# Last stage of a vision tower on one core: four orders of work changed (normalising, transposes, gather loads, low part)

## What is computed

```python
h = layer_norm(x, ln_in_g, ln_in_b)
gate = softmax((h @ router_w + router_b) / TEMP)
vals, idx = top_k(gate, 2)
mix = sum over the two chosen experts of val * (silu(h @ ew1[e] + eb1[e]) @ ew2[e] + eb2[e])
shared = (silu(h @ sw1 + sb1) @ sw2 + sb2) * 0.25
moe_out = mix + shared
fh = layer_norm(moe_out, ff_ln_g, ff_ln_b)
ff_out = silu(fh @ ff_w1 + ff_b1) @ ff_w2 + ff_b2
return x + moe_out + ff_out
```

## Time and profile before

| | us |
|---|---|
| three runs | 931.93, 933.02, 935.03 (median 933.02) |
| profiled execution | 935.13 |
| its span, first to last instruction | 933.3 |
| TensorE busy in the span | 875.3 (94%) |
| VectorE, ScalarE, GpSimd busy | 669.5, 596.8, 435.5 |
| start of the last stage's first up-projection | 798.04 |
| last matmul ends | 924.97 |

### The profile page before, as it was taken

How to read it: one execution, slowest core, us unless ns; L and a number is a source line. 1 busy time by engine, 2 the same in 40 slices (tenths; PEclk the granted TensorE clock), 3 DMA queues, 4 the chain that set the end, 5 groups by cost and what they waited for, 6 DMA issues and landing times. The chain is left out here.

```text
span 933.3 us, 22329 instructions
## 1 busy us (share of the span) xinstructions
PE 875.3 (94%) x5920; PEld 796.6 (85%) x5920; DVE 669.5 (72%) x2240; ACT 596.8 (64%) x1064; POOL 435.5 (47%) x374
## 2 busy tenths in 40 slices
PE   2999999999999999998897999999999999799996
PEld 2788888888888888887786999999999998688885
DVE  8468888787888878885755777776777774766671
ACT  3466667677776676676854666666666665567774
POOL 7012445554555555552641555665665564333330
PEclk9899999999999999999987999999999999899999
DMA  9999999999999988664167788888888873133321
GB/s 221 220 208 221 233 248 245 250 254 251 248 253 236 235 232 221 167 199 150 59 165 236 220 246 254 246 249 253 246 253 248 234 213 119 48 101 101 101 87 44
DMA packets 193915, 186.96 MB, mean 200 GB/s; under 512 B 16413, under 2 KB 168314, under 8 KB 193626
## 3 DMA queue, kind: packets, MB, share of 16 engines
q1 hardware_dynamic: 182784, 166.24, 68.2%
q0 software_dynamic: 9376, 19.42, 6.4%
q10 hardware_dynamic: 1722, 0.93, 0.5%
HBM read 150.48 MB, written 36.04 MB: 200 GB/s over the span
## 5 line engine op out<-in xcount | busy, mean ns | idle before, releaser
L1426 PE MATMUL bank<-xf,wp 128*128 128x256 f32 x1280 | 310.4, 391 | 5.4 <-ACT xf L628 5.4
L1426 PEld LDWEIGHTS bank<-xf,wp 128*128 128x128 f32 x1280 | 235.5, 190 | 47.5 <-issue 4.1
L911 POOL DMA_INDIRECT y_tok<-region,dsti x160 | 164.1, 1026 | 133.2 <-DVE region L1249 97.9
L869 POOL TENSOR_TENSOR rstd<-var,neghalf 128x4 f32<-128x4 f32 (+2 forms) x51 | 76.3, 1496 | 270.5 <-DVE var L1022 140.3
L628 ACT ACTIVATE xf<-region 128x1024 f32<-128x1024 f32 x160 | 174.0, 1136 | 19.8 <-DVE region L942 19.8
L885 POOL DMA_INDIRECT z_rows<-z,posg x130 | 157.2, 1209 | 45.5 <-issue 44.9
L1625 PE MATMUL bank<-region 128*128 128x128 f32 x1280 | 157.2, 276 | 0.0
L1625 PEld LDWEIGHTS bank<-region 128*128 128x128 f32 x1280 | 151.4, 193 | 0.0
L792 ACT ACTIVATE region<-bank,cols 128x256 f32<-128x256 f32 x320 | 126.1, 476 | 22.3 <-PE bank L1614 21.4
L1614 PE MATMUL bank<-parts 128*128 128x256 f32 x960 | 136.0, 291 | 0.3 <-DVE parts L1268 0.2
L942 DVE COPY region<-region 32x1792 f32<-32x1792 f32 x96 | 105.9, 1103 | 42.2 <-ACT hT L648 20.1
(11 more groups left out here) (179 smaller groups left out, 1213.8 us busy)
## 6 DMA issues: line engine op xcount, KB each, us to landing
region<-in_x SPq DMA_DIRECT2D x384, 196.0 KB
region<-in_L_ffn_ew SPq DMA_DIRECT2D x160, 256.0 KB
region<-z_rows SPq DMA_DIRECT2D x80, 130.0 KB, 2.7
region<-y_tok SPq DMA_DIRECT2D x16, 512.0 KB, 5.3
out<-region SPq DMA_DIRECT2D x65, 64.0 KB
ht_dram<-hT SPq DMA_DIRECT2D x16, 256.0 KB, 7.0
r_dram<-rr SPq DMA_DIRECT2D x16, 256.0 KB, 6.9
region<-ht_dram SPq DMA_DIRECT2D x16, 256.0 KB, 6.0
```

The source lines that it names most:

```text
L869: pool.tensor_tensor(dst, var, neghalf[:, 0:var.shape[1]], ALU.pow).then_inc(ready, 1)
L911: pool.indirect_dma_start(y_tok, bass.IndirectOffsetOnAxis(dsti[n % 2][:, i:i + 1], 0), yout[n % 2][:, i], None).then_inc(y_free[n % 2], 16)
L1426: ins = pe.matmul(out_cols, wp[:, s], cols_in, start=s == 0, stop=s == MAIN - 1)
```

## The change

Four places of the last stage, nothing else:

1. ACT: z_norm(q+1) stood between the first silu and the other three; it now stands ahead of all four.
2. PE: t_z(q+1) stood between the two halves of ff_down(q); it now stands between ff_up(q) and an undivided ff_down(q).
3. SP: in step q the load of group q+4 stood ahead of store_out(q); now it is the load of group q+5. The load of group 4 and that of group 5 so stand ahead of every store.
4. DVE: h4_low(q+1) stood behind out3(q-1); it now stands ahead of it.

```diff
@@ SP
             def step3(q, k, h):
-                load_gat(q + 4, k)
+                load_gat(q + 5, 1 - k)
                 store_out(q)
...
-            for q in range(2, 4):
+            for q in range(2, 5):
                 load_gat(q, q % 2)
-            groups(sp, 0, GROUPS - 4, step3)
+            step3(0, 0, 0)
+            groups(sp, 1, GROUPS - 5, step3)
             load_gat(GROUPS, 0, 1)
-            for q in range(GROUPS - 4, GROUPS):
+            for q in range(GROUPS - 5, GROUPS):
                 store_out(q)
@@ ACT
             def step3(q, k, h, z1=GT, now=GT):
-                ff_silu(q, q * EC, 0, 1, now)
                 if z1:
                     z_norm(q + 1, 1 - k, z1)
-                ff_silu(q, q * EC, 1, EC, now)
+                ff_silu(q, q * EC, 0, EC, now)
                 if z1:
                     z_in(q + 1, z1)
@@ DVE
                     norm(q + 2, m2)
+                if m1:
+                    h4_low(q + 1, m1)
                 if out:
                     out3(q - 1, 1 - k, out)
-                if m1:
-                    h4_low(q + 1, m1)
                 if m2:
                     shift(q + 2, m2)
@@ PE
             def step3(q, k, h, z1=GT, now=GT):
                 ff_up(q, now)
-                ff_down(q, k, 0, EC // 2, now)
                 if z1:
                     t_z(q + 1, z1)
-                ff_down(q, k, EC // 2, EC, now)
+                ff_down(q, k, now)
```

More of the change, by code:

```diff
@@ L1663, in ff_up, with ff_down @@
                     in_parts(bank[FF_BANK[c]][:, 0:nt * P], c, ((fw1h, h4h), (fw1h, h4l), (fw1l, h4h)), nt)
-            def ff_down(q, k, lo, hi, nt=GT):
-                if lo == 0 and not (isinstance(q, int) and q == 0):
+            def ff_down(q, k, nt=GT):
+                if not (isinstance(q, int) and q == 0):
                     pe.wait_ge(out_ready, q)
-                for c in range(lo, hi):
+                for c in range(EC):
                     pe.wait_ge(u_used, q * EC + c + 1)
@@ L1673, in ff_down @@
                                         start=c == 0 and t == 0, stop=c == EC - 1 and t == nt - 1)
-                if hi == EC:
-                    ins.then_inc(ffd_done, 1)
+                ins.then_inc(ffd_done, 1)
             pe.wait_ge(w3_loaded, 48)
```

## The result

| | before | changed kernel |
|---|---|---|
| median of 4 runs (lowest to highest), us | 932.47 (930.64 to 935.03) | 925.83 (922.31 to 927.02) |
| ratio, 95% interval | | 0.9929 [0.9908, 0.9950] |
| profiled execution, us | 935.13 | 922.31 |
| its span, us | 933.3 | 920.5 |
| first up-projection of the last stage | 798.04 | 792.49 |

The changed kernel is **6.6 us faster**. That is outside the range (928.2 to 933.7) on the low side, and on the side of "faster", to which the prediction gave 0.39.

What follows compares the result with a forecast made beforehand. Bound: two DMA engines, nearly without a hole. First packet 815.5 + 0.2, stores 96.6, loads 10.25 x 1.75 = 17.9, no holes: end 930.2 instead of 932.6, -2.4 us, so 930.6 us for the kernel; range 928.2 to 933.7.

Steps and rivals of the forecast that it cites:

- 6.82 us a step without waits: TensorE in the last stage: the length of a step once it never waits, against 7.715 before.
- +0.2 was taken: First store, out3(0) now behind h4_low(2): starts 0.2 us later, with ends of -0.3 and +2.5.
- two engines work nearly without a hole for 117.1 us: Kernel before, stores and gather loads from 815.5 to 932.6: about two DMA engines nearly always busy.
- 1.75 us a load: The two engines' share of a gather load: 19.7 us left after stores and holes, over 11.25 loads.
- 0.06: Idle holes of the two DMA engines per step in the kernel before, in us; 0.8 us in all.
- The low end of the forecast, 929.0: Whole kernel's lowest forecast time, us: first store 0.3 earlier and twice the holes that were read.
- 7.79 a step, TensorE's gain goes nowhere: Last stage: stores and load need 7.79 us a step, so 6.85 us steps build a queue; DMA sets the pace.
- one load less: SP's load ahead of the store: eleven gather loads instead of twelve in the saturated stretch, 1.75 us a load.
- TensorE sets the end: Rival: stores queue away behind, TensorE's chain sets the time, 12.7 us less, 920.3; chance 0.07.
- Half of it: Rival: holes of 0.5 us a step, not 0.06; half of the further gain, 3.5 us, giving 927; chance 0.05.
- Nothing: Rival: load 5 isn't through before the first store, or that store slips by what is saved; 933.0; chance 0.10.
- slower: Rival: out3 behind h4_low makes the first store one step (7.7 us) late; 938; chance 0.03.

Runs made afterwards that it cites:

- a_dve_undone_2: Changed kernel with DVE's part undone (sum again ahead of the low part): 923.19 us, ratio 0.9917; the same kernel on another chip 1002.32 us, 0.9981.
- a_small: Changed kernel with gather loads of one tile of each group instead of four: 997.62 us against 1005.03 before, ratio 0.9958.
- b_sp_only: Kernel before with SP's part of the change alone (load q+5 ahead of the stores of q): 930.94 us against 930.87, ratio 1.0004.
- a_tail_spread: Changed kernel with only the stores of groups 12 to 15 written as two of 64 rows x 4 tiles: 917.69 us, ratio 0.9854.
- a_sp_undone: Changed kernel with SP's part undone, only PE, ACT and DVE as changed: 934.16 us, ratio 1.0034.

## Why the prediction was wrong, point by point

**Right: the chain on TensorE.** It foresaw 6.82 us a step without waits (6.76 to 6.79 measured), the last matmul some 9 us earlier (11.4), 43 GB/s up to the end, and stores issued at 1.4 us each. The first store came 0.8 us sooner where +0.2 was taken and -0.3 was the lower end, in a first step that was 1.0 shorter. It was also right that the last stores and not TensorE end the kernel, and that part of TensorE's gain isn't paid out.

**Wrong: "two engines work nearly without a hole for 117.1 us".** This sentence is on the kernel before; it is the step that failed, and with it the 1.75 us a load. I took every slice that showed some DMA share for work at full capacity, and counted as a hole one slice, at 29 GB/s. The earlier trace rows has three more in the same step, at 38, 31 and 31 where stores alone give 44: by the same way of counting 0.3 us beside the 0.14. But a queue that is given a group each 7.7 us and needs less for it also shows packets in flight most of the time. The measured capacity, from the changed kernel (groups 0 to 10) and from a_dve_undone_2, is 7.30 us a step. Less 4 x 1.51 for the stores, that is **1.25 us a load, not 1.75**, and before the change 7.71 - 7.30, about **0.4 us of rest a step, not 0.06**. The residual of one equation was booked on the one unknown that I had named. A check was at hand in the trace: the time of SP's four issues, which doesn't grow, shown above.

That one term makes up the miss. With 1.25 for 1.75 and all else as it stands, the sum is 815.7 + 96.6 + 10.25 x 1.25 = 925.1 for the last packet, 7.5 us earlier than before, and 925.5 for the kernel, where 925.83 was measured. So the mechanism of the sum, two engines without a hole up to the end, holds for the changed kernel and not for the one before. That it comes so close is in part luck: the limit by the last sums lies at the same place (a_small), the first store was taken 1.0 us too late, and from the first store's packet to the last the trace has 110.6 us where these terms give 109.4. The low end of the forecast, 929.0, should have been about 929.3 by the terms that it names.

**Wrong for that reason: what the step would be.** "7.79 a step, TensorE's gain goes nowhere" became 6.8 for six steps and 7.0 to 7.2 for eight. VectorE wasn't waiting for gathers in the later steps, as I had announced, but for GpSimd. The term "one load less" of 1.75 measured 0 alone (b_sp_only): in that kernel the engines rest, and work taken away adds to the rest.

**What the gain is made of.** TensorE ends 11.4 us sooner: 1.0 in the first step, 10.4 in the 14 others. 4.2 are given back behind it: the distance from the last matmul to the end goes from 8.3 to 12.5. The sum of group 13 stood 13.5 us ahead of the last matmul and stands now 8.4 ahead; the sums behind it follow in 4.9 and 2.1 us where a group's stores take 6.05, and so the stores line up. Left are 7.3 us of stage, 6.6 in the medians.

**The rivals.** "TensorE sets the end" (920) had the pace right and the end wrong; a_tail_spread shows what it would have been, 917.69. "Half of it" (927) named the right doubt, holes of 0.5 us a step where I read 0.06, and came nearest to 925.83; it had 0.05, far too little, since nothing in the trace excluded it: the 0.06 was one slice in two steps. Its number is near by luck as well, since nothing but a guess made it half of the 7 us. "Nothing" and "slower" are out, but a_sp_undone shows how near the second was: without SP's part the change loses 3 us, by gathers held up behind stores and not by a late first store.

## What to carry to other kernels

That packets are in flight doesn't say that a DMA path is full: in the kernel before, fewer than two were in flight for only 1.25 of 89 us, and yet the path had about 0.4 us of rest a step. Set the time at which a group's data is ready beside the time at which its last packet passes: here a constant distance (8.3 to 8.7 us) went with a path that rested, a growing one (8.7 to 10.4) with a path that didn't; the issue time of the held-up queue (3.2 to 4.2 us for four stores, against 3.48 growing to 5.57) showed the same without counting. And a path that keeps up in the loop can still set the end: the last groups, which here come 4.9 and 2.1 us apart where a group's stores take 6.05, are where its width costs, so the last stores of a kernel are the first to be written wide (here four groups of 16 brought as much as all; that was tried only in the changed kernel, whose queue had caught up by group 13, and not in a_dve_undone, whose queue hadn't).

## What the runs showed of the hardware that I hadn't expected

- **A narrow store against a wide one.** A 64 KB store with two images as its outer dimension takes 1.51 us in a queue of such stores, which go at 43 GB/s and 0.144 of 16 engines; the same bytes with 64 rows outermost go at 180 to 208 GB/s and 0.8. A 512 KB gather, in whose burst the share reaches 0.9, costs the narrow place only 1.25 us between such stores (7.30 a group less 4 x 1.51).
- **Who gives way between VectorE and GpSimd.** VectorE's four L1320 take 1.14 us alone, and 2.13 where GpSimd's add (L927, 1.29) has just begun. But where the root of 128x4 falls on L1359, the root is the one that gets longer, by 0.47 to 0.55 us, and VectorE keeps its 0.69. The ten slow roots start 0.00 to 0.09 us behind L1359, and that L1320 (865.00 in the changed kernel) 0.09 behind the add (864.91): here what starts second gets longer. A root that starts first doesn't hold VectorE off: in the changed kernel it starts 0.16 us ahead of L1359, and neither takes longer than its 1.01 and 0.69.

```profile
891.38 1.01 POOL L869 TENSOR_TENSOR rstd<-var,neghalf 128x4 f32<-128x4 f32 x1 [3.56 <-DVE var L1350]
...
891.54 0.69 DVE L1359 TENSOR_TENSOR parts<-region,parts 128x512 fp32r<-128x512 f32 x1 [0.24 <-ACT parts L820]
```

  The root's row lasts till 892.39, and L1359 waits for ScalarE alone. The same is seen in an earlier stage of the kernel before, with a root of 128x8 and VectorE's L1036 (0.68 us in the median of 17):

```profile
461.18 1.67 POOL L869 TENSOR_TENSOR rstd<-var,neghalf 128x8 f32<-128x8 f32 x1
461.32 0.69 DVE L1036 TENSOR_TENSOR parts<-region,parts 128x512 fp32r<-128x512 f32 x1 [0.53 <-ACT parts L685]
```

  So that two such operations overlap doesn't tell that one of them gets longer; what it depends on, no run here shows.
- **The same code takes another time on another chip.** The kernel before took 930.87, 931.25 and 1005.03 us on three. On the last of them the stage of a_dve_undone took 126.28 us, and 126.48 on another; it began at 873.73 there and at 795.81 on the other, so the difference lies ahead of the last stage.
